# Feed-forward products in float on four column groups in place of three float16 products

## The reference

```
g = einsum('bsh,ehf->ebsf', x, w_gate)      # 8 experts, 128 x 512 each
u = einsum('bsh,ehf->ebsf', x, w_up)
h = silu(g) * u
expert_out = einsum('ebsf,efh->ebsh', h, w_down)
cw = router_probs * gate_weights            # two softmaxes over the experts
cw = cw / (sum(cw) + 1e-09)
out = einsum('ebsh,bse->bsh', expert_out, cw)
x = x + 0.5 * out
```

## Time and profile before

| what | value |
|---|---|
| median of 3 runs | 1571.03 us (1569.04 to 1571.74) |
| the profiled execution | 1567.27 us, its span 1565.5 us |
| PE busy | 1515.0 us, 97% |
| DVE busy | 1253.5 us, 80% |
| ACT busy | 933.7 us, 60% |
| POOL busy | 893.2 us, 57% |
| mean granted clock of TensorE | 0.993 |

### The profile page before, as it was taken

One profiled execution on the slowest core, in us unless ns is written; L12 is line 12 of the kernel. 1 busy time (PEld: TensorE's weight loads), 2 busy tenths in 40 slices (PEclk: granted clock), 3 DMA queues, 4 the chain that ended last, 5 costly groups with the idle time before them and its releaser, 6 DMA issues. The chain is left out here.

```text
span 1565.5 us, 44459 instructions
## 1 busy us (share of the span) xinstructions
PE 1515.0 (97%) x16156; PEld 918.7 (59%) x16156; DVE 1253.5 (80%) x2574; ACT 933.7 (60%) x1826; POOL 893.2 (57%) x940
## 2 busy tenths in 40 slices
PE   7999999999999999899999999999998899999998
PEld 4666666666666666666666666666663444444443
DVE  7976777767887799886777777778779989999968
ACT  7755555555555444365555555556653378888853
POOL 2855756657664255455756657657447434444455
PEclk9999999999999999999999999999999989999999
DMA  4300000000001244200000000000011212111112
GB/s 165 106 12 5 7 0 7 7 0 7 1 8 35 35 87 84 43 5 5 8 1 7 7 0 7 3 4 9 3 15 26 51 36 63 36 43 43 29 32 71
DMA packets 75264, 43.50 MB, mean 28 GB/s; under 512 B 54858, under 2 KB 71786, under 8 KB 74996
## 3 DMA queue, kind: packets, MB, share of 16 engines
q1 hardware_dynamic: 75124, 41.64, 11.5%
HBM read 10.51 MB, written 2.10 MB: 8 GB/s over the span
## 5 line engine op out<-in xcount | busy, mean ns | idle before, releaser
L662 POOL TENSOR_TENSOR scratch<-scratch 128x512 f16<-128x512 f32 x379 | 441.5, 1166 | 381.6 <-ACT scratch L900 381.3
L1470 DVE SCALAR_TENSOR_TENSOR scratch<-psum,scratch 128x512 f32<-128x512 f32 x512 | 352.5, 689 | 235.7 <-PE psum L2067 213.3
L895 ACT ACTIVATE scratch<-psum 128x512 f32<-128x512 f32 x512 | 305.2, 597 | 394.9 <-PE psum L2067 394.0
L2109 PE MATMUL psum<-ffn_down_hi,scratch 128*128 128x128 f16 x2048 | 369.3, 219 | 0.3
L2111 PE MATMUL psum<-ffn_down_hi,scratch 128*128 128x128 f16 x2048 | 369.3, 219 | 0.0
L2110 PE MATMUL psum<-ffn_down_lo,scratch 128*128 128x128 f16 x2048 | 369.3, 219 | 0.0
L900 ACT ACTIVATE scratch<-scratch 128x512 f16<-128x512 f32 x512 | 318.5, 622 | 12.1 <-DVE scratch L1470 11.9
L2109 PEld LDWEIGHTS psum<-ffn_down_hi,scratch 128*128 128x128 f16 x2048 | 200.3, 98 | 59.1 <-POOL scratch L662 0.7
L2110 PEld LDWEIGHTS psum<-ffn_down_lo,scratch 128*128 128x128 f16 x2048 | 200.3, 98 | 58.0
L2111 PEld LDWEIGHTS psum<-ffn_down_hi,scratch 128*128 128x128 f16 x2048 | 200.4, 98 | 0.0
L2065 PE MATMUL psum<-x_hi,ffn_up_hi 128*128 (+1 forms) x512 | 194.1, 379 | 2.0 <-DVE scratch L1470 2.0
(11 more groups left out here) (240 smaller groups left out, 2652.0 us busy)
## 6 DMA issues: line engine op xcount, KB each, us to landing
scratch<-scratch SPq DMA_DIRECT2D x96, 128.0 KB, 2.8
raw<-in_ffn_w_dram SPq DMA_DIRECT2D x8, 768.0 KB, 4.5
ffn_up_hi<-scratch SPq DMA_DIRECT2D x32, 128.0 KB, 2.7
x_tok<-in_x_dram SPq DMA_DIRECT2D x8, 256.0 KB, 7.3
out_dram<-x_tok SPq DMA_DIRECT2D x7, 256.0 KB, 2.0
raw<-in_lin_dram SPq DMA_DIRECT2D x1, 1092.0 KB
x_hi<-scratch SPq DMA_TRANSPOSE x46, 2.4
x_lo<-scratch SPq DMA_TRANSPOSE x46, 2.4
```

Source lines behind the costliest of these rows:

```text
L662: pool.tensor_tensor(h_lo[r], h32[r], h_hi[r], ALU.subtract).then_inc(s_plo, 1)
L895: act.activation(gate_act[k % 2], bank(k % 2), ACT.Silu, scale=W_DOWN).then_inc(s_s, 1)
L1470: dve.scalar_tensor_tensor(h32[k % HSLOTS], bank(5 + k % 2), W_DOWN, gate_act[k % 2], ALU.mult, ALU.mult).then_inc(s_h, 1)
L2109: pe.matmul(dst, h_hi[r][:, cols], hi, start=k % FC == 0 and n == 0, stop=False, skip_group_check=True)
```

## The change

The feed-forward weights are kept in float and are loaded by DMA straight to where they are used, 24 loads of 256 KB without waits between them; `split_weight` goes, on ACT and DVE. Of x a float copy `x_full` is kept, two slots of 512 columns: for blocks 0 and 1 of the first stage ACT copies it from PSUM, for all others POOL adds x_hi and x_lo (`add_halves`). h stays in float: `h_high` and `h_low` go, on ACT, POOL and DVE; `hidden` is a plain product, and the scalings by W_UP and W_DOWN go with it. Gate, up and down become `exact`: four float products, each with 32 of the 128 stationary columns, written to the four groups of 32 partitions of the same bank. The loop over blocks takes two blocks a turn, so that the slot of x_full is fixed. In block 0 the pieces of retention's tables on ACT that stood between the splits move to chunks 4 to 20, and gate and up of chunk 0 stand ahead of the router logits. The router, the other stages and the transposes are not changed.

```diff
-        ffn_g = [sb(f"ffn_gate_{h}", E * F, F16) for h in ("hi", "lo")]
-        ffn_u = [sb(f"ffn_up_{h}", E * F, F16) for h in ("hi", "lo")]
-        ffn_d = [sb(f"ffn_down_{h}", E * F, F16) for h in ("hi", "lo")]
+        ffn_g, ffn_u, ffn_d = [sb(f"ffn_{t}", E * F)[:] for t in ("gate", "up", "down")]
...
         gate_act = [carve(S) for _ in range(2)]
         h32 = [carve(S) for _ in range(HSLOTS)]
-        h_hi = [carve(S, F16) for _ in range(HSLOTS)]
-        h_lo = [carve(S, F16) for _ in range(HSLOTS)]
+        x_full = carve(2 * S)
...
             for e in range(E):
-                if e >= 2:
-                    sp.wait_ge(s_wlo, 3 * (e - 1))
-                q = e % 2
-                sp.dma_start(raw[:, 3 * F * q:3 * F * (q + 1)], ffn_w[e]).then_inc(s_wraw[q], 16)
-                if e == 0:
-                    load_x(1)
-                if e == 1:
-                    for b in range(2, NB):
-                        load_x(b)
+                for t, w in enumerate((ffn_g, ffn_u, ffn_d)):
+                    sp.dma_start(w[:, e * F:(e + 1) * F], ffn_w[e][:, t * F:(t + 1) * F]).then_inc(s_w[e // 2] if e else s_w0[t], 16)
+                if e in (0, 2):
+                    load_x(1 + e // 2)
+            for b in range(3, NB):
+                load_x(b)
...
-                def h_low(c, k, opening):
-                    if low_on_vector(k, opening):
-                        return
-                    r = k % HSLOTS
-                    pool.wait_ge(s_hhi, c + 1)
-                    pool.tensor_tensor(h_lo[r], h32[r], h_hi[r], ALU.subtract).then_inc(s_plo, 1)
+                def add_halves(b):
+                    pool.wait_ge(s_xturn, turned(n0 + SUB * (b + 1)))
+                    if not (isinstance(b, int) and b == 0):
+                        pool.wait_ge(s_u, c0 + (b - 1) * CHUNKS)
+                    pool.tensor_tensor(full(b), xseq(x_hi, b), xseq(x_lo, b), ALU.add).then_inc(s_xsum, 1)
 
...
-                        if not (last and k + 2 >= CHUNKS):
-                            h_low(c + k + 2, (k + 2) % CHUNKS, opens_late(f, b) and k + 2 < CHUNKS)
                         if opens_late(f, b):
                             rwkv(plan[ph["i"] - 1], k)
+                        if k == 4 and not last and not splits(f, b):
+                            add_halves(b + 1)
...
+                act.activation(full(b), prep_psum(at), ACT.Copy).then_inc(s_xcopy, 1)
                 act.activation(xseq(x_hi, b), prep_psum(at), ACT.Copy).then_inc(s_xhi, SUB)
...
-                    act.activation(gate_act[k % 2], bank(k % 2), ACT.Silu, scale=W_DOWN).then_inc(s_s, 1)
-
-                def h_high(c, k):
-                    act.wait_ge(s_h, c + 1)
-                    act.wait_ge(s_hfree, c + 1)
-                    act.activation(h_hi[k % HSLOTS], h32[k % HSLOTS], ACT.Copy).then_inc(s_hhi, 1)
+                    act.activation(gate_act[k % 2], bank(k % 2), ACT.Silu).then_inc(s_s, 1)
...
-                def hidden(c, q, k, first, opening=False):
+                def hidden(c, k):
                     dve.wait_ge(s_u, c + 1)
                     dve.wait_ge(s_s, c + 1)
-                    if not (first and k < HSLOTS):
-                        dve.wait_ge(s_hhi, c - HSLOTS + 1)
-                        if not low_on_vector(k, False) and not (opening and HSLOTS <= k < VECTOR_LOWS + HSLOTS):
-                            dve.wait_ge(s_plo, low_by_pool(f and not (opening and k < HSLOTS), q, k) - 3)
-                    dve.scalar_tensor_tensor(h32[k % HSLOTS], bank(5 + k % 2), W_DOWN, gate_act[k % 2], ALU.mult, ALU.mult).then_inc(s_h, 1)
-
-                def h_low(c, k, opening):
-                    if not low_on_vector(k, opening):
-                        return
-                    r = k % HSLOTS
-                    dve.wait_ge(s_hhi, c + 1)
-                    dve.tensor_tensor(h_lo[r], h32[r], h_hi[r], ALU.subtract).then_inc(s_vlo, 1)
+                    dve.wait_ge(s_hfree, c + 1)
+                    dve.tensor_tensor(h32[k % HSLOTS], bank(5 + k % 2), gate_act[k % 2], ALU.mult).then_inc(s_h, 1)
...
+            def exact(dst, lhs, rhs, first=True, last=True):
+
+                for r in range(P // 32):
+                    rows = slice(r * 32, (r + 1) * 32)
+                    ins = pe.matmul(dst[rows], lhs[:, rows], rhs, start=first, stop=last, skip_group_check=True)
+                return ins
...
+                def full_ready(b):
+                    if f == 0 and isinstance(b, int) and b < 2:
+                        pe.wait_ge(s_xcopy, b + 1)
+                    else:
+                        pe.wait_ge(s_xsum, f * NB + b - 1)
...
                     if not first:
                         pe.wait_ge(s_s, c - 1)
-                    three(bank(k % 2), part(ffn_g, k), [xseq(t, b) for t in (x_hi, x_lo)]).then_inc(s_g, 1)
+                    exact(bank(k % 2), part(ffn_g, k), full(b)).then_inc(s_g, 1)
 
                 def up(c, k, b, first):
                     if not first:
                         pe.wait_ge(s_h, c - 1)
-                    three(bank(5 + k % 2), part(ffn_u, k), [xseq(t, b) for t in (x_hi, x_lo)]).then_inc(s_u, 1)
-
-                def down(c, q, k, opening):
-
-                    if low_on_vector(k, opening):
-                        pe.wait_ge(s_vlo, low_by_vector(f, q, k, opening))
-                    else:
-                        pe.wait_ge(s_plo, low_by_pool(f, q, k))
-                    r, e = k % HSLOTS, k // FC
-                    hi, lo = part(ffn_d, k)
+                    exact(bank(5 + k % 2), part(ffn_u, k), full(b)).then_inc(s_u, 1)
+
+                def down(c, k):
+
+                    pe.wait_ge(s_h, c + 1)
+                    e = k // FC
                     for n in range(SUB):
-                        dst = bank(2 + e % 2, n * P, (n + 1) * P)
                         cols = slice(n * P, (n + 1) * P)
-                        pe.matmul(dst, h_hi[r][:, cols], hi, start=k % FC == 0 and n == 0, stop=False, skip_group_check=True)
-                        pe.matmul(dst, h_hi[r][:, cols], lo, start=False, stop=False, skip_group_check=True)
-                        ins = pe.matmul(dst, h_lo[r][:, cols], hi, start=False, stop=k % FC == FC - 1 and n == SUB - 1, skip_group_check=True)
+                        ins = exact(bank(2 + e % 2, n * P, (n + 1) * P), h32[k % HSLOTS][:, cols], part(ffn_d, k),
+                                    k % FC == 0 and n == 0, k % FC == FC - 1 and n == SUB - 1)
                     ins.then_inc(s_hfree, 1)
...
+                        full_ready(0)
+                        pe.wait_ge(s_w0[0], 16)
+                        gate(c0, 0, 0, True)
+                        pe.wait_ge(s_w0[1], 16)
+                        up(c0, 0, 0, True)
                         pe.wait_ge(s_frlo, 1)
-                    logits(r0, 0)
-                    for k in range(2):
-                        if f == 0 and k == 0:
-                            pe.wait_ge(s_wlo, 1)
-                        if f and k == 1:
-                            pe.wait_ge(s_y8, NB)
-                            pe.wait_ge(s_ysq, NB)
-                        gate(c0 + k, k, 0, not f)
-                        if f == 0 and k == 0:
-                            pe.wait_ge(s_wlo, 2)
-                        if f == 0:
-                            up(c0 + k, k, 0, True)
+                        logits(r0, 0)
+                        gate(c0 + 1, 1, 0, True)
+                        up(c0 + 1, 1, 0, True)
+                    if f:
+                        logits(r0, 0)
+                        full_ready(0)
+                        gate(c0, 0, 0, False)
+                        pe.wait_ge(s_y8, NB)
+                        pe.wait_ge(s_ysq, NB)
+                        gate(c0 + 1, 1, 0, False)
                 if 2 in start:
                     if f:
                         for k in range(2):
...
                     pe.wait_ge(s_rout, NB)
 
-                def body(b, last):
+                def body(b, odd, last):
                     c, q = c0 + b * CHUNKS, q0 + b * E
                     static = isinstance(b, int)
                     for k in range(CHUNKS):
                         kk = k + AHEAD
-                        bk = b + kk // CHUNKS
+                        bk = (odd + kk // CHUNKS) % 2
                         if splits(f, b) and kk < CHUNKS and kk % FC == 0:
-                            pe.wait_ge(s_wlo, 3 * (kk // FC) + 2)
+                            pe.wait_ge(s_w[kk // FC // 2], 16 * 3 * min(kk // FC, 2))
                         if kk == CHUNKS and not last:
-                            x_ready(b + 1)
+                            full_ready(b + 1)
                         if kk < CHUNKS or not last:
                             gate(c + kk, kk % CHUNKS, bk, False)
                             up(c + kk, kk % CHUNKS, bk, False)
                         if k == 1 and not last:
                             logits(r0 + b + 1, b + 1)
```

(65 more changed lines are left out.)

67 lines of the change are left out of this document (14 added, 53 removed).

## The result

The changed kernel takes 1906.74 us (1901.74 to 1910.75, four runs) against 1570.03 for the kernel before beside it: a ratio of 1.214, 95% interval 1.211 to 1.218. Forecast were 1897 us and a range of 1862 to 1935. Its profiled execution, the fastest of the four, has a span of 1900.0 us, 334.5 more than before.

The account below looks back on a forecast made before the run. PE's streamed columns were taken to bound the feed-forward. Chunk +320, router visits +4, retention pieces +5, opening -3 and the POOL step 0 gave +326 us on 1571.03, hence 1897 us, range 1862 to 1935.

Parts of the forecast that it names:

- What bounds: Feed-forward stages: bound by the columns PE streams, 1.965 us a chunk; relief of the other engines is worth nothing there.
- The chunk, 2.59 us: Feed-forward chunk on PE: from 1.965 to 2.59 us, 512 times, +320 us (+284 to +340).
- the form changes for the router: Router logits, once a block: PE leaves the float column groups and returns, 0.27 us a visit, 16 visits, +4 us.
- The opening, -3: From 12.47 to 86.85 us: PE idle partly covered as splits go and the h chain shortens; -3 us (-4.4 to +3).
- Pieces of the retention stage, +5: Last block of first feed-forward, first of second: retention pieces between down products cost form changes, 0 to +8, taken +5 us.
- rival B: Every product pays the fixed part, or instructions issue too slowly at a steady rate: chunk 2.88 us, kernel 2048 us; 4%.
- The signs of being wrong: Blocks below 81 or above 85 us, clock leaving 1.00, PE idling there, or stages after second feed-forward changing by several microseconds.
- A: Clock rival: PE at 1.2 GHz throughout the float chunks, 5.2 us a chunk, kernel about 3220 us; 5%.
- C: One shared moving tensor streams at one cycle a column: chunk 1.30 us, kernel about 1265 us, faster than before; 3%.
- D: The four products of a group do not overlap: 10.4 us a chunk, kernel over 5800 us; 1%.

Follow-up runs that it names:

- experiment 5: Changed kernel with gate, up and down all in the old float16 shapes on constant data, feed-forward values left out: 1573.16 us, ratio 1.0017 to the kernel before.
- experiment 2: Changed kernel with each float product done once on the whole array in place of four column groups, same result: 1896.72 us.
- experiment 3: Changed kernel with gate and up as three float16 products each on constant data, down still in float on column groups: 1803.72 us.
- experiment 6: The kernel before with PE's loop going through two blocks a turn, nothing else changed: 1576.49 us, ratio 1.0044 to the kernel before.
- experiment 4: Changed kernel with down as twelve float16 products on constant data, gate and up still in float on column groups: 1914.56 us.

## Why the prediction was right, point by point

**What bounds.** PE's stream in the feed-forward. Right: PE is busy throughout all undisturbed blocks before and after, and experiment 5 takes the whole loss away by giving PE's old shapes back and nothing else.

**The chunk, 2.59 us by the earlier trace rows.** Measured 2.59; block 83.41 against 83.2. The rows of two other stages carried it, once the fixed part of a visit was told from the streaming by comparing widths and by taking a chain. With the form changes for the router, 16 x (83.41 - 63.18) = +323.7, forecast 324: +320 by the chunk and 0.22 us for each visit, where I had 0.27. Experiments 2 and 3 split a visit: 0.12 to 0.13 us on leaving the column groups, which the whole array does not pay, and 0.08 to 0.10 on coming back to float, which it pays too. The Trainium skill, TensorEngine Tiling (Array Packing), Key Properties, says that a change of tiling mode drains TensorE; the trace agrees for the step out of the column groups, shows no cost between products of one form, and has the step back cost about the same where no tiling changes.

**The opening, -3.** The first down starts at 22.56 (21.33 before) and block 0 has lost its 2.34 us over an undisturbed one: -1.1. From block 15 to the end -2.1 us more. The gates and ups of three chunks (3 x 0.42 = 1.26 us more than before) are done ahead of the first down and are missing in block 15; set against each other, the opening itself is 2.4 us better and the end 0.9. The size is right. Whether the shorter chain did it, as I wrote, stays open: in experiment 5 the chain is as short and block 0 takes 65.81 us (65.52 before), but there the clock was at 1.2 GHz from 21.7 to 25.1 us.

**Pieces of the retention stage, +5.** Wrong in size, +0.2: from block 7's first down to block 8's +19.96, block 8 itself +20.73, against 20.23. Each visit costs its 0.25 (periods of 3.26 became 4.13, where 0.62 is the longer chunk), but where PE had waited for DVE between the pieces (3.66 became 3.05) the longer chunk covers it. I had counted the visits and not the waits.

**Not in the sum: the turn of PE's loop, +13.8.** The largest miss. I named the loop over pairs as part of the change and gave it no price, and in rival B I asked whether PE's instructions come fast enough only as a steady rate, which they do. 323.7 - 1.1 + 0.2 - 2.1 + 13.8 = 334.5, the difference of the spans. My sum was 326, 8.5 short: the 13.8 were left out, and the 5 for the pieces hid a third of that, which was luck. With the turn in and the 5 out the forecast would have been 1906.

**The signs of being wrong.** Three of those that I had named did show, and all at the turn: one block of each stage took 88.2 and 90.6 us, PE idled there, and the granted clock left 1.00. They rightly pointed at a step that the prediction lacked, although the time lies in its range.

**Rivals.** A: the clock is at 2.4 GHz in all undisturbed blocks of float products, so sustained float keeps it; in the profiled execution it fell at the two turns, where PE had stood still, and for some 20 us from 1579 us, as it had from 1245 us before. B: the fixed part comes with a change of form and not with a product. (My 2048 for it left out the 0.06 that I had named for each small product; with it the chunk is 3.12 and the time about 2170.) C: one shared moving tensor streams no faster than four. D: the four overlap.

## What to carry to other kernels

A float32 product of 128 rows took four cycles a moving column here (0.86 us for 512 columns at 2.4 GHz), against three for three float16 products (0.65 us); where PE's stream is the bound, float in place of a three-way split makes that stream a third longer, however much it relieves the others. Price a new form from a chain of it or from two widths, never from one isolated visit. And when a change makes a loop's body longer, price its turn: write the loop out or keep the body short.

## What I had not expected of the hardware

- PE's branch back took 0.22 us with a body of about 1150 records and 3.4 to 4.7 us with bodies of 2350 and more; with the same work for PE, the packets of the instruction queue rose from 87 to 131 (experiment 6). With about 1600 it took 0.24 us in one stage and 3.47 in the other, so where the limit lies, and whether it is length alone, stays open.
- How much of the branch is seen differs with the kernel: of 3.47 us 0.33 at 24 records a chunk (experiment 2), of 3.4 to 3.8 us 1.7 to 2.0 at 36, of 3.9 us 3.3 and more at 96. That fits queued work covering the rest, since longer records hold more of it; the queue itself was not varied alone. In the second stage of the changed kernel PE stopped a second time after one pass of the next gate, for 2.2 us (5.6 us of its 8.9 are there), and experiment 4 did the same in its second stage (1.4 and 2.5 us). Why the refill came in two parts there was not tried.
- The stall costs more than itself: the clock was at its lower level for 3.4 and 6.8 us after the changed kernel's turns. It did not always fall: after the second turn in experiments 5 and 6, where PE had idled 1.97 and 1.74 us, and after the first in experiment 3, where it had idled 2.84, it stayed at the upper one.
- Four column groups of 32 and the whole array of 128 stream a float product of 512 columns at the same rate (0.86 us). The small one is 0.22 in both, by the chunks (2.59 and 2.61 us) some 0.005 us longer on the whole array.
